# Layer 0 of a four-layer megakernel: masked decay factors from a product scan on VectorE instead of differences and masks on Pool

## The reference, cut to what matters

```python
q = rmsnorm(x @ Wq); k = rmsnorm(x @ Wk); v = rmsnorm(x @ Wv)
gt = jax.nn.log_sigmoid(x @ Wgt) / 16.0
...
bc = jnp.cumsum(g, axis=-1)                      # g: gt within a chunk of 64
decay = jnp.exp(bc[..., :, None] - bc[..., None, :])
mask = jnp.tril(jnp.ones((c, c), dtype=bool))
A = einsum('bhnid,bhnjd->bhnij', q, k) * jnp.where(mask, decay, 0.0)
o_intra = einsum('bhnij,bhnjd->bhnid', A, v)
```

## Time and profile before

| what | value |
| --- | --- |
| median of 3 runs | 1984.92 us (1975.03 to 1997.05) |
| the profiled execution | 1989.19 us; its span 1986.7 us |
| busy: PE, DVE, ACT, POOL | 1739.2 us (88%), 1499.5 us (75%), 1425.6 us (72%), 1501.3 us (76%) |
| mean granted TensorE clock | 0.942 |

### The profile page before, as it was taken

How to read it: one execution, slowest core, us unless ns; L and a number is a source line. 1 busy time by engine, 2 the same in 40 slices (tenths; PEclk the granted TensorE clock), 3 DMA queues, 4 the chain that set the end, 5 groups by cost and what they waited for, 6 DMA issues and landing times.

```text
span 1986.7 us, 44726 instructions
## 1 busy us (share of the span) xinstructions
PE 1739.2 (88%) x13639; PEld 1045.9 (53%) x13639; DVE 1499.5 (75%) x2777; ACT 1425.6 (72%) x3297; POOL 1501.3 (76%) x1215
## 2 busy tenths in 40 slices
PE   6779878878988757987999999999999999998897
PEld 3447556555656525634644644644644644644554
DVE  4653664665555442998899999989989989988896
ACT  4557666657667436687788788788788788787674
POOL 1742783584486422889989989989989989988996
PEclk9789889889989867998999999999999999999899
DMA  9224336335425566333633633633643644542530
GB/s 290 68 82 128 72 102 176 85 100 150 103 81 152 120 167 198 81 114 112 159 113 104 168 113 111 161 115 114 156 120 111 155 123 118 144 138 87 150 86 22
DMA packets 162137, 245.78 MB, mean 124 GB/s; under 512 B 32712, under 2 KB 107112, under 8 KB 161904
## 3 DMA queue, kind: packets, MB, share of 16 engines
q1 hardware_dynamic: 149616, 226.15, 40.4%
q0 software_dynamic: 12288, 16.79, 4.1%
HBM read 169.39 MB, written 73.47 MB: 122 GB/s over the span
## 4 chain that ended last, share of the span: by engine, by line
PE 35%; POOL 12%; issue 8%; DVE 4%; DMA 2%; ACT 2%; SPq 1%; POOLq 0%; DVEq 0%; ACTq 0%
PE bank L2291 31%; POOL HB L2236 7%; POOL HB L2242 4%; PE bank L2394 2%; DVE bank L2790 1%; DVE HB L2790 1%; PE bank L2422 1%; POOL SD L2262 1%; PE bank L2300 1%; SPq L2167 0%; DMA X<-x_scratch 0%; DMA us_scratch<-SD 0%; DMA out<-X 0%; DVE nmax L2814 0%; DMA dd_scratch<-U 0%
## 5 line engine op out<-in xcount | busy, mean ns | idle before, releaser
L2236 POOL TENSOR_TENSOR HB<-DD,BC 128x512 f32<-128x512 f32 x512 | 642.9, 1280 | 81.8 <-PE bank L2291 58.8
L2582 ACT ACTIVATE bank<-DD,A 128x512 f32<-128x512 f32 x512 | 352.0, 692 | 111.6 <-DVE HB L2795 56.9
L2790 DVE TENSOR_TENSOR_SCAN bank<-bank,HB 128x512 f32<-128x512 f32 x256 | 311.6, 1217 | 35.2 <-ACT bank L2582 18.9
L2242 POOL TENSOR_TENSOR HB<-HB,BC 128x512 f32<-128x512 f32 x256 | 324.2, 1280 | 14.7 <-DVE HB L2790 14.7
L2790 DVE TENSOR_TENSOR_SCAN HB<-bank,HB 128x512 f32<-128x512 f32 x256 | 310.6, 1213 | 20.7 <-POOL HB L2236 17.1
L2795 DVE TENSOR_TENSOR HB<-bank,BC 128x512 f32<-128x512 f32 x256 | 175.8, 687 | 14.8
L2291 PE MATMUL bank<-HB,fold 128*32 128x512 f32 x1024 | 139.4, 616 | 33.8 <-POOL HB L2242 18.6
L711 POOL DMA_INDIRECT X<-expert_out_scratch,slot x64 | 100.5, 1570 | 85.0 <-DMA expert_out_scratch<-YS 60.7
L2394 PEld LDWEIGHTS bank<-ident,PR 128*128 128x128 f32 x768 | 90.4, 145 | 74.8 <-issue 44.4
L2394 PE MATMUL bank<-ident,PR 128*128 128x128 f32 x768 | 117.3, 285 | 11.2 <-ACT PR L2620 9.6
L2291 PE MATMUL bank<-XRT,Wk 128*128 128x512 f32 x256 | 123.3, 607 | 3.7 <-ACT Qa L2596 3.7
(11 more groups left out here) (286 smaller groups left out, 3985.3 us busy)
## 6 DMA issues: line engine op xcount, KB each, us to landing
DD<-dd_scratch SPq DMA_DIRECT2D x512, 128.0 KB, 3.4
ROW<-row_scratch SPq DMA_DIRECT2D x64, 256.0 KB
BC<-ssm_scratch SPq DMA_DIRECT2D x128, 128.0 KB, 5.2
US<-us_scratch SPq DMA_DIRECT2D x32, 512.0 KB, 5.2
XL<-sorted_scratch SPq DMA_DIRECT2D x92, 128.0 KB, 2.5
expert_out_scratch<-YS SPq DMA_DIRECT2D x92, 128.0 KB, 1.8
us_scratch<-U SPq DMA_DIRECT2D x8, 1024.0 KB, 4.2
us_scratch<-SD SPq DMA_DIRECT2D x8, 1024.0 KB, 6.8
```

The lines of the kernel that those rows point to most:

```text
L2236: done(pool.tensor_tensor(HB[:, c % HR], du, bc, ALU.mult), "dbu")
L2242: done(pool.tensor_tensor(h, h, bc, ALU.mult), "cg")
L2582: done(act.activation(PD[n % 2][:], delta, ACT.Exp, scale=A[:, k:k + 1]), "dA")
L2790: done(dve.tensor_tensor_scan(h if n % 2 else dA, dA, h, 0.0, ALU.mult, ALU.add), "scan")
```

## The change: what it does

The masked decay factors of a tile are no longer made from sums. `sr` now only transposes the gates; `src` (ScalarE) takes their exp into `BR`, except for the first token of each chunk, whose place stays at the zero written once at the start. `ROW` is then a row of factors exp(gt), zero at each chunk's first token. A new step `dc` on VectorE makes `dec` in one instruction for each tile: a scan over 128x1024 elements that goes through the row as state = ROW[i] * state + own_token[i], where `own_token` is one at the key's own token and zero elsewhere. So the state is zero up to the key's own token, one there, and the running product behind it. The steps `df`, `md` (Pool), `de`, `vs` (ScalarE) and `suc` (VectorE) are gone, 136 in all, and 32 `dc` are new: the list has 3040 steps instead of 3144.

The step `v1` moves from VectorE to ScalarE. The squares of the values are now taken in `vgc`, from the PSUM bank and not from `VG`. A few waits change with this, and the whole table `L0_ORDER` is replaced.

```diff
-EXP_STEPS, SILU_STEPS = {"ga", "gx", "er", "de", "rf", "hr"}, {"sg", "si"}
+EXP_STEPS, SILU_STEPS = {"ga", "gx", "er", "src", "rf", "hr"}, {"sg", "si"}
...
                 def rows_load(b, t):
                     sp.wait_ge(over["row_st"], 16 * (b + 1))
-                    after(sp, "de", *lag(b, t, 2, NT))
+                    after(sp, "dc", *lag(b, t, 2, NT))
...
-                def differences(b, t):
-                    after(pool, "suc", b, 0)
-                    pool.wait_ge(over[f"row_in{t % 2}"], 64 * b + 32 * (t // 2 + 1))
-                    done(pool.tensor_tensor(ROW[:, t % 2], ROW[:, t % 2], bc(COL[:, t], CH), ALU.subtract), "df")
-
-                def mask_later(b, t):
-                    after(pool, "df", b, t)
-                    done(pool.tensor_tensor(ROW[:, t % 2], ROW[:, t % 2], mid(later[:], H), ALU.add), "md")
...
-                def sum_rows(b):
+                def turn_gates(b):
                     after(pe, "gl", b, 0)
-                    first(pe, b, "consts", CONSTS)
                     bank = claimed(pe, "sr", b, 0)
                     for t in range(NT):
-                        q = mm(bank[0:H, t * P:(t + 1) * P], gt[:, t], prefix[:])
+                        q = pe.transpose(bank[0:H, t * P:(t + 1) * P], gt[:, t], ident[:])
                     done(q, "sr")
...
+                def scaled_values(b, t):
+                    after(act, "fk", b, 0)
+                    after(act, "vgc", b, t)
+                    after(act, "o", b - 1, 2 * t, 2 * t + 1)
+                    first(act, b, "zeros", ZEROS)
+                    done(act.activation(own_slots(v1[:, t]), pairs(VG[:, t, 0:D]), ACT.Copy, scale=fkv[:, t:t + 1]), "v1")
...
-                def sums_row(b):
+                def factor_rows(b):
+
                     after(act, "sr", b, 0)
+                    first(act, b, "zeros", ZEROS)
                     if b:
                         act.wait_ge(over["row_st"], 16 * b)
-                    done(act.activation(BR[0:H], banks.of["sr", b, 0][0:H], ACT.Copy), "src")
-
-                def decay(b, t):
-                    after(act, "md", b, t)
-                    bb, tt = lag(b, t, 2, NT)
-                    after(act, "at", bb, *range(4 * tt, 4 * tt + 4))
-                    done(act.activation(dec[:, t % 2], ROW[:, t % 2], ACT.Exp), "de")
+                    chunks = "h (n i) -> h n i"
+                    done(act.activation(BR[0:H].rearrange(chunks, i=CH)[:, :, 1:],
+                                        banks.of["sr", b, 0][0:H].rearrange(chunks, i=CH)[:, :, 1:], ACT.Exp), "src")
...
                 def gates(b, t):
                     after(act, "vg", b, t)
                     after(act, "v1", b - 1, t)
-                    after(act, "vs", b - 1, t)
                     after(act, "sg", b - 1, t)
-                    done(act.activation(VG[:, t], banks.of["vg", b, t][:], ACT.Copy), "vgc")
+                    src = banks.of["vg", b, t][:]
+                    act.activation(VG[:, t], src, ACT.Copy)
+                    after(act, "ou", b - 1, t)
+                    squared(b, t, 2, src[:, 0:D], v2[:, t], "vgc")
...
-                def scaled_values(b, t):
-                    after(dve, "fk", b, 0)
-                    after(dve, "vgc", b, t)
-                    after(dve, "o", b - 1, 2 * t, 2 * t + 1)
-                    done(dve.tensor_scalar(own_slots(v1[:, t]), pairs(VG[:, t, 0:D]), fkv[:, t:t + 1], None, ALU.mult), "v1")
...
+                def decays(b, t):
+
+                    dve.wait_ge(over[f"row_in{t % 2}"], 64 * b + 32 * (t // 2 + 1))
+                    first(dve, b, "consts", CONSTS)
+                    bb, tt = lag(b, t, 2, NT)
+                    after(dve, "at", bb, *range(4 * tt, 4 * tt + 4))
+                    flat = "p h i -> p (h i)"
+                    done(dve.tensor_tensor_scan(dec[:, t % 2].rearrange(flat), ROW[:, t % 2].rearrange(flat),
+                                                own_token[:].rearrange(flat), 0.0, ALU.mult, ALU.add), "dc")
```

Of the table, one row stands for the rest (the numbers are places in the one list of steps, one for each batch):

```diff
-    "src": [60, 115, 333, 815, 1120, 1599, 1885, 2404],
+    "src": [51, 106, 352, 863, 1049, 1603, 1840, 2372],
```

More of the change, by code:

```diff
@@ L642, in constants @@
                     for t, v in ((half, -0.5), (suffix, 1.0), (prefix, 1.0), (chunk0, 1.0), (chunk1, 0.0),
-                                 (later, -1e30), (before, 1.0)):
+                                 (own_token, 0.0), (before, 1.0)):
                         own(pool.memset(t[:], v))
@@ L656, in constants @@
                     for c in range(2):
-                        own.now(pool.affine_select(out=later[c * CH:(c + 1) * CH], in_=later[c * CH:(c + 1) * CH],
-                                                   compare_op=ALU.is_gt, fill=0.0, base=0,
-                                                   pattern=[[-1, CH]], channel_multiplier=1))
+                        own.now(pool.affine_select(out=own_token[c * CH:(c + 1) * CH], in_=own_token[c * CH:(c + 1) * CH],
+                                                   compare_op=ALU.not_equal, fill=1.0, base=0,
+                                                   pattern=[[0, H], [-1, CH]], channel_multiplier=1))
                     own.now(pool.affine_select(out=before[:], in_=before[:], compare_op=ALU.is_gt, fill=0.0, base=0,
@@ L1097, in row_factors @@
                     after(act, "kc", b, *range(NT))
-                    after(act, "vs", b, *range(NT))
+                    after(act, "vgc", b, *range(NT))
                     after(act, "fk", b - 1, 0)
@@ L1180, in _ @@
                         scaled_queries_turned(b, i)
+                    elif what == "v1":
+                        scaled_values(b, i)
                     elif what == "oe":
@@ L1456, in row_stats @@
                     after(dve, "rp", b - 1, t)
+                    after(dve, "xn", b - 1, t)
                     own.now(dve.bn_stats(st[:, t], X[:, b % 2, t]))
@@ L1496, in _ @@
                         log_gates(b)
-                    elif what == "suc":
-                        sum_columns(b)
                     elif what == "gm":
```

89 lines of the change are left out of this document (36 added, 53 removed), and 342 rows, old and new, of the table L0_ORDER.

## The result

The changed kernel takes 1917.6 us (median of 4 runs, 1913.3 to 1920.0); the kernel before, run beside it on the same chip, 1991.0 (median of 4, 1975.0 to 2001.2). The ratio is 0.963, with a 95% interval of 0.958 to 0.968: faster by 73 us, where 31 were forecast and the range ended at 63.

The account below looks back on a forecast made before the run. No engine was full; TensorE, the fullest in layer 0, was kept waiting and then partly ran at the low clock. Terms -4 - 22 + 7 - 6 - 9 + 3 = -31 took 1984.9 to 1954 us; range 1922 to 1984.

Parts of the forecast that it names:

- The clock: TensorE in layer 0: less work at the low clock after its long waits, -9 us, bounds 0 and -45.
- Holds and clock, -22 and -9: Layer 0: VectorE no longer held by Pool, so TensorE waits less, -22 us; less TensorE work at low clock, -9.
- Pool, -4: df and md leave Pool's queue ahead of the last group's scaling and scattering: -4 us, bounds 0 and -9.
- VectorE's own work: Layer 0: 32 scans of 2.26 us may stand ahead of what TensorE needs: +7 us, bounds 0 and +22.
- The start: Layer 0's first batch: VectorE waits for row broadcasts until some 50 us, delaying other work: +3 us, bounds -4 and +14.
- ScalarE, -6: Layer 0: de and 21 table loads leave ScalarE, v1 comes; mostly covered by idle time: -6 us, bounds 0 and -15.
- TensorE, 0: Layer 0: four transposes replace four products of the same size, 0 us.
- the next one was late: Rival: other operands arrive just behind the removed waits, so half of each gain is lost: 1975 us, chance 0.20.
- The scan isn't held: Rival claimed the opposite: VectorE's scan and Pool's scaling hold each other, +12 us on the forecast: 1966 us, chance 0.08.
- VectorE waits for rows: Rival: Pool's wait for row broadcasts moves to VectorE at 8 batches, +70 us: slower, 2024 us, chance 0.08.
- The holder is no other: Rival claimed the opposite: Pool's scatters and gathers hold VectorE, so the holds stay: 1997 us, chance 0.04.

Follow-up runs that it names:

- the fills: The kernel before, with Pool's df and md replaced by memsets of about the same length that read nothing, same order and waits: 1922.6 us, ratio 0.979.

## Why the prediction was wrong

The first cause was right, and so were its place and its view: Pool's reads held VectorE, and the holds went. What failed is the size of what follows from them. Two readings say it, one of the profiles and one of the runs.

By the two profiles of layer 0, the forecast's terms other than the clock come to -22 (-4 - 22 + 7 - 6 + 3), and TensorE stands still for 40 us less. The clock was put at -9 and is worth 15 to 27, and the transposes, put at 0, took 5 us off TensorE's busy time. So the step **The clock** is the one most clearly mis-sized: I priced it only behind the long waits that I had found, while the mean clock of the whole stretch rose. Its own bound, -45, held. The range did not keep to the bounds: its lower end took 37 us of waits and 26 of the clock and left out those of Pool, -9, and of ScalarE, -15, with which it would have been 1898, below what was measured.

By the runs, part by part:

- **Holds and clock, -22 and -9.** Measured together by the fills, in the old order: 2.1%, 41 us, with an interval of some 30 to 53. The forecast's 31 is at its lower end. I had counted the longest wait of each of four releasers and left the many small ones; that this is the difference is not shown.
- **Pool, -4.** The steps' waits were worth 18 us (some 5 to 30), their 144 us of busy time nothing. I had priced the busy time of one pair at the end, and no wait. Twice the bound of -9.
- **VectorE's own work, +7, bounds 0 and +22.** In the old order 35 us, above the bound: a block of 2.3 us stands ahead of things that TensorE needs half the time, while I had taken the rate of the holds, 0.31, and then a third of it. In the new order, the one that was forecast, 0, the lower bound. The reason that I gave for the low value, "well ahead of its `at` at most places", was read from the new list and is right for it; but the price then wasn't carried to its end.
- **The order, no term.** It takes 2.4% off the new work and nothing off the old. Some 35 of its 46 us are the scans, hidden, if their second half costs what the first does; for the other 11 no run has a cause, though the start below, the place of the squares and the three waits may be part of it. Of the 42 us that the forecast missed the hidden scans are only the 7 above, since it had put them near to covered.
- **The start, +3.** VectorE did stand 8.6 us for the rows, as forecast, but the first `AT` came 16 us earlier. In the kernel before the first decays were ready at 61 us (the first row, of ScalarE's timeline), and the first `AT` came at 73.7, having waited for its bank only 0.54 us. What kept it was VectorE's list, in which it stood behind expert choice and the first states, and holds among these, one of 2.40 us:

```profile
59.92 1.06 ACT L1054 ACTIVATE dec<-ROW 128x1024 f32<-128x1024 f32 x1
```

```profile
62.39 2.40 DVE L1424 TENSOR_TENSOR S<-sdec,kvm 128x64 f32<-128x64 f32 x1
...
73.71 1.42 DVE L1395 TENSOR_TENSOR AT<-bank,dec 128x256 f32<-128x256 f32 x4 [0.54 <-PE bank L740]
```

The new list has the first four at steps 113 to 129, ahead of expert choice's ranks from 137 on; the old one at 178 to 185, behind them from 128 on. In the old order with the new work it came at 68.5 us (VectorE, one line), and with the old work in the new order at 70.0, so it takes both. I had looked at what the rows let begin and not at what stood in the list behind them. How much of the 16 us reaches the end is not isolated.

```profile
L1270 DVE TENSOR_TENSOR AT<-bank,dec x128: 407/415/426, 68.5 to 632.3; 128x256 f32<-128x256 f32 x128
```

- **ScalarE, -6, bound -15.** From the new order without Pool's steps (0.971) to the changed kernel (0.959 to 0.963): 16 to 24 us for the decays and table loads that left ScalarE, with scans that cost nothing. It is a remainder between runs of different groups, and it holds also what my placing of the old steps in the new order cost, so I only say that it is at the bound or past it. `v1`, which came to ScalarE, costs nothing there: taken back to VectorE it moved no time.
- **TensorE, 0.** The transposes are not products of the same size to TensorE: 32 matmuls for 64, 5 us less. Whether that reached the end was not tested.

With these sizes, -41 for holds and clock, -18 for Pool, 0 for the scans and -16 to -24 for what is left, the sum is -75 to -83 for the 73 measured. That is no proof of them: the first two are of the old order, and the last is a remainder. In the old order -41 - 18 + 35 = -24, and the run has 24 to 28, but most of that agreement is made, since the terms come from differences of the same runs; only the 35 has a source of its own, the halved scans. That the forecast's -31 is near to that kernel's time is chance.

The rivals: the next one was late in small things only (AT's waits grew by 5 us), and the gain was twice the forecast and not half. The scan isn't held (2282 ns in the median, 2478 at most), and what it holds, Pool's scaling, is not on the path: with scans of half the length it shrank and the time stayed. VectorE waits for rows once. The holder is no other: writes by Pool of the same length set the two-input instructions free.

## What to carry to other kernels

Before an operation is moved to another engine, ask what else its old engine's reads were stopping: a few held instructions of 2 us can cost more than the operation's own time, and a read/write exchange of the same length prices that by itself. When a change brings a new order of steps, price the new blocks in that order and compare it with the old one; "covered" and "half on the path" were about 35 us apart here with the same instructions. An engine that is half idle can still be the one that may not get anything more: in the new order 161 us more of Pool cost half of themselves, while in the old one some 148 us of fills cost no more than short ones in their place. And where waits go, price the clock over the whole stretch and not only behind the longest waits.

## What was not expected of the hardware

- Fills by Pool leave VectorE's two-input instructions free (236 ns) and hold TENSOR_SCALAR (637 in the mean for a median of 368; 390 with fills of 64 elements).
- A scan holds Pool as Pool held VectorE: the scaling went from 948 to 1379 ns in the mean, and back to 1165 with half scans.
- The kernel before takes 1958 to 1960 us in some groups of runs and 1988 to 1991 in others, and it is not the chip: on the one numbered 13 it took 1959.7 us in one group and 1990.3 and 1988.5 in two later ones. The changed kernel shows where: layer 1 begins at 645.1 us in one run and at 604.5 in the other, and lasts 1269 and 1273. I have no cause for it.

```profile
L2195 POOL MEMSET first<- x1: 106/106/106, 645.1 to 645.1; 128x8 f32 x1
```

```profile
L2195 POOL MEMSET first<- x1: 105/105/105, 604.5 to 604.5; 128x8 f32 x1
```
